# A deformable convolution's closing addition, moved from behind tap 0 to behind tap 1 of the next chunk

## What is computed

```python
x = x + deform(gn(x))        # layer 0
x = x + ternary_block(gn(x)) # layer 1

def deform(x):               # 3x3, 9 taps
    om = conv3x3(x, w_off) + b_off        # 27 maps: 9 x (dy, dx), 9 masks
    # each tap reads x bilinearly at its own shifted place, times sigmoid(mask)
    return einsum('bckhw,ock->bohw', sampled, w_conv)

def ternary_block(x):
    out1 = relu(batchnorm(conv3x3(x, ternary(w1))))
    return relu(out1 + batchnorm(conv3x3(out1, ternary(w2))))
```

## Time and profile before

| | |
|---|---|
| time, median of 3 runs | 2828.99 us (2826.62 to 2830.62) |
| the profiled execution | 2835.05 us, span 2833.3 us |
| granted TensorE clock, mean over the span | 0.929 |
| busy share of the span | TensorE 84%, VectorE 79%, ScalarE 46%, GpSimd 49% |
| 16 DMA engines, mean over the span | 293 GB/s |
| the five stages with deformable work and the first convolution | to about 2250 us of the span |

### The profile page before, as it was taken

The page is one execution under the profiler, slowest core; times in us unless marked ns, Lnnn a source line. Parts: engine busy times, 40 slices in busy tenths (PEclk is TensorE's granted clock), DMA queues, the critical chain, the costliest instruction groups (busy, mean ns, idle before and its releaser), DMA issues. The chain is left out here.

```text
span 2833.3 us, 38210 instructions
## 1 busy us (share of the span) xinstructions
PE 2391.2 (84%) x12442; PEld 1714.7 (61%) x12442; DVE 2237.7 (79%) x4777; ACT 1295.3 (46%) x2245; POOL 1374.5 (49%) x1262
## 2 busy tenths in 40 slices
PE   4599888868989999899999998888888869999930
PEld 3355555535555666566666665555555869999930
DVE  7688988977878888788788887888886865566665
ACT  3455445445545455455455444444443333333345
POOL 1465656645555556555565655666664003333300
PEclk8799999989999999999999999999999989999965
DMA  8999999988989999989899998999997321111179
GB/s 287 369 358 364 365 357 336 369 288 314 352 325 360 361 350 344 340 322 359 334 359 355 345 340 313 354 350 338 346 343 263 127 72 55 58 56 56 37 303 408
DMA packets 279391, 831.09 MB, mean 293 GB/s; under 512 B 25916, under 2 KB 59708, under 8 KB 278468
## 3 DMA queue, kind: packets, MB, share of 16 engines
q0 software_dynamic: 165888, 604.05, 56.9%
q1 hardware_dynamic: 113348, 225.20, 22.5%
HBM read 743.67 MB, written 85.48 MB: 293 GB/s over the span
## 5 line engine op out<-in xcount | busy, mean ns | idle before, releaser
L479 POOL DMA_INDIRECT G<-pixel_pairs,quad_c x1152 | 1212.3, 1052 | 873.4 <-PE psT L1236 566.9
L1003 DVE SCALAR_TENSOR_TENSOR G<-G,wts_c 128x256 f32<-128x256 f32 (+1 forms) x2304 | 1256.0, 614 | 154.8 <-DMA G<-pixel_pairs,quad_c 151.1
L1149 PE MATMUL psD<-ST,wconv 128*128 128x512 f32 x2304 | 1087.4, 617 | 0.0
L1149 PEld LDWEIGHTS psD<-ST,wconv 128*128 128x128 f32 x2304 | 438.9, 201 | 445.1 <-issue 445.1
L584 ACT ACTIVATE G<-G,wts_c 128x256 f32<-128x256 f32 x1152 | 489.9, 497 | 477.2 <-DVE G L1003 476.4
L1236 PE MATMUL psT<-idn,G 128*128 128x128 f32 x2304 | 333.1, 292 | 232.5 <-ACT G L584 230.7
L643 ACT ACTIVATE ST<-psT 128x1024 f32<-128x1024 f32 x288 | 294.3, 1022 | 463.9 <-PE psT L1236 463.2
L1236 PEld LDWEIGHTS psT<-idn,G 128*128 128x128 f32 x2304 | 281.1, 150 | 303.5 <-ACT G L584 200.5
L1137 PE MATMUL psF<-pl,qw 128*128 128x256 f32 x1872 | 262.6, 294 | 13.4 <-DVE pl L842 10.8
L1137 PEld LDWEIGHTS psF<-pl,qw 128*128 128x128 f32 x1872 | 238.9, 190 | 38.1 <-issue 17.9
L1549 PE MATMUL psG<-po,qw 128*128 128x256 f32 x1440 | 227.8, 287 | 25.0 <-POOL po L1400 25.0
(11 more groups left out here) (220 smaller groups left out, 2434.8 us busy)
## 6 DMA issues: line engine op xcount, KB each, us to landing
xx<-in_x SPq DMA_DIRECT2D x56, 512.0 KB, 5.0
pixel_pairs<-yT SPq DMA_DIRECT2D x104, 256.0 KB, 6.8
G<-pixel_pairs,quad_c POOLq DMA_INDIRECT x1152, 6.7
x<-x1c SPq DMA_DIRECT2D x32, 512.0 KB, 5.3
h<-h1c SPq DMA_DIRECT2D x32, 512.0 KB, 8.6
out<-h SPq DMA_DIRECT2D x16, 1024.0 KB, 17.1
xf<-x SPq DMA_DIRECT2D x24, 640.0 KB, 8.9
area<-h SPq DMA_DIRECT2D x24, 640.0 KB, 4.0
```

The costliest lines, as they stand in the source:

```text
L479: pool.indirect_dma_start(out=G[:, i % RING, :], out_offset=None, in_=tbl[d.b].rearrange("y x q c -> (y x) (q c)"), in_offset=bass.Indirec ...
L1003: dve.scalar_tensor_tensor(g[:, 0:w], g[:, w:2 * w], wts_c[:, d.p, q * NG + i:q * NG + i + 1], g[:, 0:w], ALU.mult, ALU.add).then_inc(d_ma ...
L1149: ins = pe.matmul(psD[:, oc, :], wconv[:, t, k, oc * 128:(oc + 1) * 128], ST[:, k % 3, t, :], start=(k == 0 and t == 0), stop=(k == TAPS - ...
```

## The change

One condition in the emission of VectorE: the call of `finish_deform` for chunks 1 to 7 stands behind tap 1's multiply-adds instead of tap 0's.

```diff
@@ -1003,7 +1003,7 @@
                                     dve.scalar_tensor_tensor(g[:, 0:w], g[:, w:2 * w], wts_c[:, d.p, q * NG + i:q * NG + i + 1],
                                                              g[:, 0:w], ALU.mult, ALU.add).then_inc(d_mac, 1)
                                 dve.memset(pause[:, 2 * k + q - 1:2 * k + q], 0.0)
-                            if k == 0 and not d.first:
+                            if k == 1 and not d.first:
                                 finish_deform(d.b, d.r - 1, d.n - 1, 1 - d.p, d.half if d.p else d.half - 1)
                         if k == 0 and f and f.first:
                             finish_deform(s - 1, NR - 1, f.n + NR - 1, 1, f.half + NR // 2 - 1)
```

## The result

The changed kernel takes **2814.12 us** (median of 4 runs, 2809.51 to 2815.11), the kernel before on the same chip 2829.80 us (4 runs, 2826.62 to 2840.31): a ratio of 0.9935, 95% interval 0.9907 to 0.9963. It is faster by 16 us where 48 us were forecast. The profiled execution of the change took 2809.51 us, span 2807.7 us, granted clock 0.930.

A forecast was written before the change was run, and what follows sets the result against it. VectorE and TensorE were taken to wait for each other in turn at chunk boundaries, because the addition stands between taps 0 and 1. Gains of 25 + 15 + 8 = 48 us gave 2781 us, range 2754 to 2816.

The forecast's parts named there:

- stage 3's 25 us: Seven boundaries of stage 3: TensorE's 3.63 us wait at tap 1 won, taken as 3.6 us each, 25 us.
- 58 were forecast: Sign in stage 3: its chunks should take 58 us and move 366 GB/s.
- TensorE's stop at tap 1: Sign: TensorE's wait at tap 1 should be gone in stages 1 to 3.
- stage 3's wait ahead of tap 3: Sign: TensorE's wait ahead of tap 3 in stage 3 should still be near 4.2 us.
- a stop stands ahead of tap 3 as forecast: Sign in stages 1 and 2: TensorE stops about 3 us ahead of tap 3 in place of 0.46.
- forecast 8: Stage 0, seven boundaries: between nothing and 16.1 us, half taken, 8 us.
- forecast 15: Stages 1 and 2, fourteen boundaries: between nothing and 29.9 us, half taken, 15 us.
- the two terms: Gains forecast outside stage 3: 8 us for stage 0 and 15 us for stages 1 and 2.
- VectorE's wait ahead of line 866: Sign: VectorE's wait for TensorE's convolutions falls from 111.8 us to about 25, nearly all of it in stage 3.
- the three conditions named as making it wrong: Stage 3 under 357 GB/s; tap 1's transposes still waiting for ScalarE; gather waits growing over half the other wait's loss.
- The transfers are full already: Rival: no stage passes 357 GB/s, stage 3 gives 14.5 us, the others nothing: 2814 us; chance 0.20.
- Slower: the transfers fall on tap 4's gathers: Rival, stages 0 to 2: transfers behind the addition delay tap 4's gathers, VectorE stops 3.9 us per chunk: 2886 us; chance 0.06.

The follow-up runs named there:

- the timed run of stage 3 alone: Kernel before with the addition moved behind tap 1 in stage 3 alone (7 of 28 places): 2828.88 us, ratio 0.9991.
- the two with transfers late everywhere: Load of x's rows and store of x1 put behind tap 5's transposes in every stage: on the change 2811.91 us, on the kernel before 2860.74 us.
- The timed run of these stages alone: Kernel before with the addition moved behind tap 1 in stages 0, 1 and 2 alone (21 places): 2812.76 us, ratio 0.9935.
- the late transfers: Kernel before with load of x's rows and store of x1 behind tap 5's transposes in every stage: 2860.74 us, ratio 1.0108.
- behind tap 6 in stage 3 alone: Kernel before with load of x's rows and store of x1 behind tap 6's transposes in stage 3, first chunks excepted: 2831.93 us, ratio 1.0.
- the fastest version: The change with load of x's rows and store of x1 behind tap 6's transposes in stage 3, first chunks excepted: 2798.55 us, ratio 0.9884.
- the two edits: In stage 3, addition behind tap 1, and x-row load and x1 store behind tap 6's transposes: alone 0.9991 and 1.0 against the kernel before.
- the change with filled stops: The change with unread extra matmuls ahead of tap 3's and tap 5's transposes in stage 3, chunks 1 to 5: 2810.72 us, ratio 0.9921.

## Why the prediction was right and wrong

**The step that failed** is stage 3's 25 us: "So VectorE allows 4.3 us and the gathers 4.0 us", and for the transfers as a whole "they allow 369.5 x (1 - 343/368) = 25 us: just enough". It measured 0.6 us by the windows, and nothing that can be told from none by the timed run of stage 3 alone (ratio 0.9991, by its interval at most 5.7 us). Two things were wrong in it. The chain was followed as far as tap 3 and then taken as won. As far as that it holds: tap 3's transposes come at +17.1 in place of +20.5, 3.4 us of the 3.6. But for stage 3 tap 4's gathers, one tap further on, were left out: they are issued 2.2 us sooner and land when they had landed before (+20.5 and +20.4), and TensorE loses 2.00 us in the stop behind them and 1.70 us in a slow convolution. The prediction names these gathers only as a rival for stages 0 to 2. And the transfers' room was worked out from means over a stage and a chunk. The room was there, as 409.6 us in place of 431.2 for seven chunks shows, or 58.5 us a chunk where 58 were forecast; but it was there only with other transfers taken out of the stretch in which these gathers are on their way. 25 us forecast, 21.6 us in the profile once the transfers follow.

**Right, by its own marks.** TensorE's stop at tap 1 is gone in stages 1 to 3 (in stage 0, 1.5 us of the 5.39 are left), and at the boundary shown stage 3's wait ahead of tap 3 is 4.69 us (forecast near 4.2). In stage 1 a stop stands ahead of tap 3 as forecast (2.9), with slow transposes and a slow convolution behind it; in stage 2 it is shorter, 1.1 to 2.8 us by the trace:

```profile
976.94 1.97 PE L1236 MATMUL psT<-idn,G 128*128 128x128 f32 x8 [3.32 <-ACT G L584]
978.70 4.27 PE L1149 MATMUL psD<-ST,wconv 128*128 128x512 f32 x8
```

**Right in size.** By the table, and as the mean of the five kernels with the change's code in stages 0 to 2 against the three without (the two with transfers late everywhere left out), stage 0 gave 10 us (461.8 to 451.7; forecast 8) and stages 1 and 2 together 11 (470.3 to 463.6 and 454.5 to 450.4; forecast 15). The timed run of these stages alone gives 18 us (2830.76 less 2812.76) against the 23 of the two terms.

**Right for a wrong reason.** VectorE's wait ahead of line 866 was to be about 25 us and is 22.4, but the 25 were to lie in stage 3, where six chunks have 3.4. The prediction's own working had tap 1 done 0.2 us before the addition could begin, so that mark was inconsistent; and 12.4 of the 22.4 us are the last addition of all. In stage 3 the old wait became one for gathers, tap 1's and tap 4's above all (20.3 to 45.5 us in all).

**Two of the three conditions named as making it wrong came true:** stage 3 stayed at 344 GB/s, under 357; and the wait for gathers grew by 49.8 us, 56% of the 89.4 that the other wait lost.

**The rivals.** "The transfers are full already" gave 2814 us, the time measured, but not by its mechanism: it let stages 0 to 2 gain nothing and stage 3 14.5 us, and it was the other way round. Nor does 357 GB/s bound a stage: stage 0 of the change ran at 365 GB/s for 379.7 us. By the Trainium skill, DMA: Bandwidth & Descriptors, "Where 436 GB/s comes from", HBM gives one core about 358 GB/s, and this binds between HBM and SBUF; the trace exceeds that here. The Trainium skill, HBM Reference, "Specifications (TRN2)", says that a core streaming alone measures well above that share, and this case's one core agrees, with 398 to 406 GB/s over 20 us. "Slower: the transfers fall on tap 4's gathers" had the right place, tap 4, but the wrong price. In stages 0 to 2 tap 4's gathers took about 4 us longer to land, not 6.4 (the slowest of four, median of seven chunks: 7.0, 7.6 and 7.2 us before, 10.7, 11.7 and 11.4 after), and VectorE waits 31 us for them in 21 chunks where it had not waited at all. That is 1.5 us a chunk, above the 1.2 us from which this rival was to decide, and yet these stages became 21 us shorter: a wait of VectorE there is not time of the chunk. In stage 3, which the rival left out, tap 4 and what followed cost the 3.7 us that tap 1 had won.

**What stays open:** how the 30 us that the late transfers cost the kernel before come about chunk by chunk, since behind tap 6 in stage 3 alone VectorE's waits for gathers grow as well (24 to 37 us in seven chunks) and nothing is lost; what, besides the first chunks, cost the change the 13 us that it lost elsewhere when they were late in all stages (15.0 won in stage 3, 2.2 by the medians); and how much of tap 4's late landing is the earlier store of h1, which no run held back. A stop of 4.2 us ahead of tap 3 remains in the fastest version.

## What to carry to other kernels

When a wait is removed between two engines, follow the chain to the place where the loop closes (the same tap one chunk on), and ask at each step when its transfers are issued, not only how long they took before: while the DMA engines were full, a gather that was asked for 2.2 us sooner landed no sooner. Judge the room of full DMA engines in stretches as short as the wait in question, since a stage's mean share of 0.93 was 1.02 and 0.77 side by side here. If a moved step collides with transfers that are not urgent, try to move those as well, and look at what they meet in their new place: in stage 3 the two edits were worth nothing each that could be told, and together about 15 us.

## What was not expected of the hardware

A slow stretch of TensorE stood behind several of its stops, but not behind all of them. In windows of 5 us (columns as above), the kernel before has one behind the stop at tap 3, and the change has one behind the same stop (clock 0.73 in the window from 1943.7, above) and a second one behind the new stop at tap 5:

```profile
1970.70:1975.70 5.00, 4.51 (x12) 2.97 (x13) 5.00 (x11) 5.00 (x8) 1.42 (x2) 0.50 0.89 353
```

```profile
1958.70:1963.70 5.00, 5.00 (x14) 2.66 (x15) 5.00 (x12) 2.73 (x5) 3.37 (x4) 0.66 1.02 392
```

A granted clock of 0.50 is the lower level, 1.2 GHz; 0.73 and 0.66 are parts of a window at either level. A stop of 2.00 us cost 1.70 us more in the convolution behind it, nearly as much as a stop of 4.18 us did before (5.48 less 3.60, at 1972.95 in the trace of before), whose transposes were slow as well. But behind the 3.63 us ahead of tap 1 the kernel before has a convolution at full speed, and so has the change with filled stops behind its 1.76 us:

```profile
1959.10 3.60 PE L1149 MATMUL psD<-ST,wconv 128*128 128x512 f32 x8
```

So the length of a stop alone doesn't say whether a slow stretch follows; what does, no run here shows. And the DMA engines moved more than any mean of a stage shows: 410 GB/s over 5 us of the change, and 406 over 20 us in the fastest version.
